# Attention: the order of the operations inside a step, on TensorE and on the engines that serve it

## What is computed

```python
qkv = x @ qkv_w.T + qkv_b
q = _apply_rope(q, cos, sin); k = _apply_rope(k, cos, sin)
logits = jnp.einsum('bqhmd,bkhd->bhmqk', q, k) * SM_SCALE        # 256 x 256 per head, masked to the window
w = e / (jnp.sum(e, axis=-1, keepdims=True) + exp_sink)          # e = exp(logits - max)
out = jnp.einsum('bhmqk,bkhd->bqhmd', w, v).reshape(Bv, Tv, N_HEADS * HEAD_DIM)
return out @ out_w.T + out_b
```

## Time and profile before

| | us |
|---|---|
| median of three runs | 1990.8 |
| the profiled execution | 1991.15 |
| its span in the profile | 1989.3 |
| a window of sweep 0 (305.40 to 352.10, unit of step 3 to unit of step 3) | 46.70 |
| a window of sweep 1 (905.36 to 951.85, the same L834 instruction) | 46.49 |
| TensorE busy over the span | 1945.1 (98%) |
| VectorE, ScalarE, GpSimd busy | 1549.4, 932.2, 826.0 |

### The profile page before, as it was taken

One profiled execution on the slowest core, in us unless ns is written; L12 is line 12 of the kernel. 1 busy time (PEld: TensorE's weight loads), 2 busy tenths in 40 slices (PEclk: granted clock), 3 DMA queues, 4 the chain that ended last, 5 costly groups with the idle time before them and its releaser, 6 DMA issues.

```text
span 1989.3 us, 44846 instructions
## 1 busy us (share of the span) xinstructions
PE 1945.1 (98%) x15500; PEld 1601.7 (81%) x15500; DVE 1549.4 (78%) x4948; ACT 932.2 (47%) x3481; POOL 826.0 (42%) x947
## 2 busy tenths in 40 slices
PE   6899999999999999999999999999999999999899
PEld 6688888888888888888888888888887777777687
DVE  5777777777777777777777777777777899999887
ACT  4554555555555555555555555555544222222333
POOL 3444434333333333333333333333332666666554
PEclk9999999999999999999999999999999999999999
DMA  6146211111112122121111111111104533333343
GB/s 213 46 118 142 72 54 55 65 54 55 55 54 75 44 97 76 55 89 62 54 55 54 54 54 55 54 65 54 54 33 167 183 103 93 93 93 93 106 142 121
DMA packets 71538, 162.20 MB, mean 82 GB/s; under 512 B 6656, under 2 KB 15232, under 8 KB 71184
## 3 DMA queue, kind: packets, MB, share of 16 engines
q1 hardware_dynamic: 62720, 142.48, 21.4%
q0 software_dynamic: 3840, 8.39, 2.3%
q10 hardware_dynamic: 4752, 8.46, 1.1%
HBM read 108.96 MB, written 50.41 MB: 80 GB/s over the span
## 4 chain that ended last, share of the span: by engine, by line
PE 91%; DVE 3%; issue 2%; ACT 2%; POOL 1%; DMA 0%; DVEq 0%; SPq 0%; ACTq 0%; POOLq 0%
PE banks L534 22%; PE banks L596 18%; PE banks L1180 16%; PE banks L573 9%; PE banks L549 9%; PE banks L559 6%; PE banks L1408 5%; PE banks L527 4%; ACT pr L673 1%; PE banks L484 1%; PE banks L1398 1%; PE banks L473 1%; PE banks L1392 1%; DVE pr L891 1%; DVE m L867 0%
## 5 line engine op out<-in xcount | busy, mean ns | idle before, releaser
L673 ACT ACTIVATE pr<-pr,mx 128x128 f32<-128x128 f32 x1024 | 399.0, 391 | 353.1 <-DVE mx L891 353.0
L752 POOL TENSOR_TENSOR m<-m,rope_sb 128x512 f32<-128x512 f32 x160 | 206.3, 1289 | 513.9 <-ACT m L660 513.9
L534 PE MATMUL banks<-xTh,wh 128*128 128x256 f32 x1280 | 376.4, 294 | 2.3 <-DVE xTl L851 1.4
L534 PE MATMUL banks<-xTl,wh 128*128 128x256 f32 x1280 | 363.0, 284 | 0.0
L534 PE MATMUL banks<-xTh,wl 128*128 128x256 f32 x1280 | 362.6, 283 | 0.0
L1180 PE MATMUL banks<-kv,tap 128*128 128x288 f32 x1280 | 318.4, 408 | 4.3 <-issue 1.5
L1180 PEld LDWEIGHTS banks<-kv,tap 128*128 128x128 f32 x1280 | 238.1, 190 | 83.9 <-issue 23.3
L534 PEld LDWEIGHTS banks<-xTh,wh 128*128 128x128 f32 x1280 | 246.2, 192 | 4.0 <-DVE xTl L851 1.8
L900 DVE TENSOR_TENSOR den<-ac,es 128x4 f32<-128x4 f32 x256 | 51.7, 202 | 253.9 <-ACT es L676 253.7
L534 PEld LDWEIGHTS banks<-xTl,wh 128*128 128x128 f32 x1280 | 246.5, 193 | 0.0
L534 PEld LDWEIGHTS banks<-xTh,wl 128*128 128x128 f32 x1280 | 246.1, 192 | 0.0
(11 more groups left out here) (110 smaller groups left out, 3825.6 us busy)
## 6 DMA issues: line engine op xcount, KB each, us to landing
tap<-padded_taps SPq DMA_DIRECT2D x64, 256.0 KB, 3.3
kk<-in_ctxt SPq DMA_DIRECT2D x64, 192.0 KB, 3.4
x_in<-in_x SPq DMA_DIRECT2D x16, 512.0 KB, 3.8
xt_split<-xTh SPq DMA_DIRECT2D x16, 512.0 KB, 2.6
xt_split<-xTl SPq DMA_DIRECT2D x16, 512.0 KB, 3.6
xb<-in_x SPq DMA_DIRECT2D x16, 512.0 KB, 4.6
factors<-in_factors POOLq DMA_DIRECT2D x8, 1024.0 KB, 8.6
x_part_rows<-x SPq DMA_DIRECT2D x16, 512.0 KB, 3.0
```

The costliest lines, as they stand in the source:

```text
L534: last = pe.matmul(bank[:, h * T:(h + 1) * T], w[:, n, c, h * P:(h + 1) * P], a[:, s, c, :], start=(c == 0 and i == 0), stop=(c == KD - 1 ...
L673: act.activation(pr[:, s, a, cols], pr[:, s, a, cols], ACT.Exp, bias=mx[:, s, i:i + 1], scale=-1.0, accum_out=ac[:, s, i:i + 1])
L752: pool.tensor_tensor(m2[:, s], m2[:, s], rope_sb[:, 1 if i == 0 else 0, 1:3], ALU.mult).then_inc(sin_ready, 1)
```

## The change

```diff
--- before.py
+++ after.py
@@ -279,6 +279,10 @@
 
     def unit_of(p, j):
         return UNIT_AT.get(2 * (p % 4) + j)
+
+    def begun(y, p):
+
+        return not (y.first and p < 4)
 
     def unit_bank(y, p, n):
 
@@ -605,21 +609,25 @@
         def body(y):
             for p in range(8):
                 for j in range(2):
+                    n = unit_of(p, j)
                     if y.here(p, 3):
                         p_transposes(y, p, j)
-                    n = unit_of(p, j)
-                    if n is not None and not y.drain:
+                    if n is not None and not begun(y, p):
                         unit(y, p, n)
-                    if x_next(y, p, j):
+                    if x_next(y, p, j) and not begun(y, p):
                         x_transposes(y.window(p) + 1, p % 4 - 1)
                     if j == 0 and y.here(p, 2):
                         scores(y, p)
                     u, jj = (p - 4, 1) if j == 0 else (p - 3, 0)
                     if y.here(u, 0):
                         pv(y, u, jj)
+                    if x_next(y, p, j) and begun(y, p):
+                        x_transposes(y.window(p) + 1, p % 4 - 1)
                     if x1_here(y, p, j) is not None:
                         x1_transposes(y.window(p) - 3, x1_here(y, p, j),
                                       (QM + 1) * 2 * B if y.drain else (QM + 1) * y.window(p) + 1 + p % 4)
+                    if n is not None and begun(y, p) and not y.drain:
+                        unit(y, p, n)
                     if y.drain and p == 3 and j == 1:
                         conv.first_products(pe)
                     for s in parts_of(y, p, j):
@@ -707,23 +715,25 @@
                     if y.here(p, 3):
                         p_evac(y, p, j)
                     n = unit_of(p, j)
-                    if n is not None and n != V_UNIT and not y.drain:
+                    if n is not None and n != V_UNIT and not begun(y, p):
                         bent(y, p, rope_index(n), unit_bank(y, p, n))
-                    if x_next(y, p, j):
+                    if x_next(y, p, j) and not begun(y, p):
                         x_high(y.window(p) + 1, (p // 4 + 1) % 2, p % 4 - 1, y.m + p // 4)
                     u, jj = (p - 4, 1) if j == 0 else (p - 3, 0)
-                    if y.here(u, 0):
+                    if y.here(u, 0) and (j == 0 or not begun(y, p)):
                         o_high(y, u, jj)
+                    if y.here(p, 2):
+                        exps(y, p, j)
+                    if y.here(u, 0) and j == 1 and begun(y, p):
+                        o_high(y, u, jj)
+                    if x_next(y, p, j) and begun(y, p):
+                        x_high(y.window(p) + 1, (p // 4 + 1) % 2, p % 4 - 1, y.m + p // 4)
                     if x1_here(y, p, j) is not None:
                         x1_evac(y.window(p) - 3, x1_here(y, p, j))
-                    if not y.first:
-                        for i, n in split_now(y, p, j):
-                            split_high(i, n)
-                    if y.here(p, 2):
-                        exps(y, p, j)
-                    if y.first:
-                        for i, n in split_now(y, p, j):
-                            split_high(i, n)
+                    if n is not None and n != V_UNIT and begun(y, p) and not y.drain:
+                        bent(y, p, rope_index(n), unit_bank(y, p, n))
+                    for i, n in split_now(y, p, j):
+                        split_high(i, n)
                 if y.drain and p in (4, 6):
                     conv.first_queries(act, p // 2 - 2)
                 if y.drain and p == 4:
@@ -781,18 +791,20 @@
             for p in range(8):
                 for j in range(2):
                     n = unit_of(p, j)
-                    if n is not None and n != V_UNIT and not y.drain:
+                    if n is not None and n != V_UNIT and not begun(y, p):
                         rotate(y, p, rope_index(n))
+                    if y.here(p, 2):
+                        if y.first and p == 2 and j == 0:
+                            pool.wait_ge(c_in, 16 * NCONST)
+                        sinks_shifted(y, p, j)
                     if p % 4 == 1 and j == 0 and not y.first and not late(y, 2, p):
 
                         pool.wait_ge(xb_landed, 16 * (y.window(p) - 1))
                         for t in range(NT):
                             last = pool.tensor_tensor(xb[:, t, :], xb[:, t, :], bo_sb[:], ALU.add)
                         last.then_inc(xb_ready, 1)
-                    if y.here(p, 2):
-                        if y.first and p == 2 and j == 0:
-                            pool.wait_ge(c_in, 16 * NCONST)
-                        sinks_shifted(y, p, j)
+                    if n is not None and n != V_UNIT and begun(y, p) and not y.drain:
+                        rotate(y, p, rope_index(n))
                     for i, n in split_now(y, p, j):
                         if y.first and n >= NU:
                             split_low(i, n)
@@ -965,15 +977,19 @@
                         conv.first_sums(dve)
                     if residual_tile(y, p, j) is not None:
                         residual(y, p, residual_tile(y, p, j))
+                    if j == 1 and begun(y, p) and y.here(p, 2):
+                        mask_min(y, p, j)
                     u, jj = (p - 3, 1) if j == 0 else (p - 2, 0)
                     if y.here(u, 0):
                         divide(y, u, jj)
                     if y.here(p, 3):
                         mask_transposed(y, p, j)
+                    if j == 0 and begun(y, p) and y.here(p, 2):
+                        mask_min(y, p, j)
+                    u, jj = (p - 4, 1) if j == 0 else (p - 3, 0)
+                    if y.here(u, 0) and begun(y, p):
+                        o_low(y, u, jj)
                     n = unit_of(p, j)
-                    early = 2 * (p % 4) + j in (1, 3) and not fresh(y, p) and not y.drain
-                    if early:
-                        mask_min(y, p, j)
                     if n is not None and not y.drain:
                         if y.first and n == V_UNIT and p < 4:
                             dve.wait_ge(c_in, 16 * NCONST)
@@ -983,10 +999,9 @@
                             turned(y, p, rope_index(n), unit_bank(y, p, n))
                     if x_next(y, p, j):
                         x_low(y.window(p) + 1, (p // 4 + 1) % 2, p % 4 - 1)
-                    if y.here(p, 2) and not early:
+                    if y.here(p, 2) and not begun(y, p):
                         mask_min(y, p, j)
-                    u, jj = (p - 4, 1) if j == 0 else (p - 3, 0)
-                    if y.here(u, 0):
+                    if y.here(u, 0) and not begun(y, p):
                         o_low(y, u, jj)
                     sl = 2 * (p % 4) + j
                     if sl in (4, 6) and x_after(y, p):
```

## The result

The changed kernel takes 2120.97 us in the median (2120.13 to 2122.66) against 1990.32: 1.0659 times the time before, 95% interval 1.0645 to 1.0672. The profiled execution is at 2120.13, 129.0 over the profiled one of before; the sum had said 117.

The account below looks back on a forecast made before the run. TensorE, busy 98% of the span, was taken as the bound. The sum 14 × 5.1 − 2 + 4 × 1.3 + 5 + 13 × 2.9 = 117 over 1991.15 gave 2108 us, range 2040 to 2140.

Parts of the forecast that it names:

- The short way from the key unit to the next: Shared bank, steps 0 to 1: next unit due after 4.29, bank read takes 5.10, so 0.81 wait a window.
- The hold of `rotate` on `divide`: VectorE beside GpSimd: `divide` is held until `rotate` ends, the next start at `bent` + 4.04, not + 2.82.
- The first rival: `rotate` doesn't hold `divide` on VectorE: 29 us of loss, 2020 us; chance 14%.
- The replay of a window: Steady sweep 0 window: units of steps 1, 3, 5 wait 2.77, 1.66, 1.02; window 51.79, 5.1 more than before.
- In step 7 the values' `v_evac` ... fits in 4.29: Step 7, bank of the values unit: `v_evac` needs 0.68 only and fits in the 4.29 to the next unit.
- Sweep 1: Windows of the second sweep: waits of 1.46 in step 1 and 1.6 in step 3; 49.40, 2.9 more each.
- The seams: TensorE, where one kind of matmul follows another: 8 us to gain over 32 windows, with PV 0.45 behind transposes.
- Window 1 has waits of its own that hide some: 2 off: Window 1: waits already there hide some of the new loss, so 2 us are taken off the sum.
- `split_high` behind `bent` ...; I take 5: Ten steps: `split_low`, first on VectorE in the next step, comes later; nothing or 1.2 each, taken as 5 us.
- The second rival: VectorE's chain also delays step 0's transposes and `o_low` before PV: about 1 per window in 27 windows, 2135 us; 11%.

Follow-up runs that it names:

- e4: The changed kernel with VectorE's `mask_min` ahead of `divide` in even steps too; 2041.41 us, 1.0257 times before.
- e1: The changed kernel with `rotate`'s two GpSimd instructions cut from 512 to 4 columns a partition after the first body; 2045.62 us, 1.0278 times before.
- e9: e4, but PV of step 7 takes the values of the window before and waits for those alone; 2026.13 us, 1.0178 times before.
- e11: e4 with e7's two edits, output projection parts moved from step 7 to the next step 0 and from step 5 to step 6; 2001.09 us.
- e7: The changed kernel with window 1 in the old order and `split_high` ahead of `exps`; 2108.91 us, 1.0592 times before.
- e8: The kernel before, sweep 0's x transposes moved behind PV, `x_high` behind `o_high`, `x_low` behind `o_low`, from window 2 on; 2010.22 us, ratio 1.0098.
- e6: e4 with the old order in step 6 alone, on all engines; 2063.82 us, 1.0365 times before.
- e5: e4 with the old order in steps 0 and 6, on all engines; 2084.42 us, 1.0467 times before.
- e10: e4 with e7's two edits, output projection parts moved from step 1 to step 0 and from step 5 to step 6; 2026.96 us, 1.0181 times before.

## Why the prediction was right

The time lies in the range and 13 us above the value, 130.7 of loss where 117 was forecast. By its own steps:

- **The short way from the key unit to the next** (0.81): right. It is 0.81 in e4 and 0.83 in e1, where everything else is out of its way.
- **The hold of `rotate` on `divide`** (`bent` + 4.04): right, 4.00 in the trace. e1 takes it away and 75 us with it; e4 takes it away together with 1.6 of VectorE's queue, and 80 us. It is three products of eight that are held, not four: in step 2 it is `den`. The Trainium skill (GPSIMD Engine Reference, Key points) names contention between GpSimd and instructions of VectorE with two SBUF inputs, without a price; the trace of after agrees, with 1.63 for an instruction that takes 0.69 alone. The first rival falls.
- **The replay of a window:** waits of 2.77, 1.66 and 1.02 forecast, 1.98, 1.28 and 0.76 measured, and one of 0.46 that the replay didn't have. "In step 7 the values' `v_evac` ... fits in 4.29" looked at the unit of step 7 alone; PV of step 7 multiplies with this window's values and comes before that unit. e9 prices it at 15 us. `bent` of step 7 starts 0.31 before step 0 (309.08 against 309.39), not 0.38 after it, and these 0.69 make up most of the 0.79 by which the wait in step 1 is smaller. That the helpers catch up while TensorE stands at PV fits this, but was not tried. In sum 4.35 a window where I had 5.1.
- **Sweep 1:** waits of 1.46 and 1.6 forecast, 1.13 and 1.11 measured, and three that the replay didn't have: 0.46 at PV of step 7, 0.33 at PV of step 3, 0.2 at the transposes of step 2. In sum 3.36 a window where I had 2.9: the two named waits were too high, and what was left out made up for it.
- **The seams** ("8 us to gain"): mis-sized. Transposes to PV are 0.53, the upper bound, not 0.45; a unit behind PV is 2.97 and a part behind it 1.39, near enough. Taking the four waits from the window of sweep 0 leaves 46.58, and e11 says 46.67 in sweep 1 and 46.66 in sweep 0: no gain, where 8 us were in the sum.
- **"Window 1 has waits of its own that hide some: 2 off":** wrong in sign. Windows 0 and 1 lose 9.3, not 3.1. e7 returns it there, 4.2 of it not for good. The sum has no term for the granted clock, and up to 6 of the 9.3 can be that.
- **"`split_high` behind `bent` ...; I take 5":** too low. Windows 15 to 18 lose 20.7, against 10.2 with this term in it. The step that failed is that it was priced as `split_low`'s length in ten slack steps. In windows 16 and 18 the split stands in front of `divide` in step 0, at the head of the chain that reaches the unit of step 1, which starts 8.1 and 8.0 after the key unit. Then the clock falls, which adds 3.8. e7 returns 6 of the 20.7; how the rest divides between `split_low` and the clock was not tried.

The last two and windows 19 to 31 are low by about 23 in all, with 2 at the end, windows 2 to 14 high by about 13. The loss was right to 12% partly by luck: errors of both signs met.

The second rival (transposes of step 0 and `o_low` late as well) did not come as it was put: the transposes of step 0 don't wait in steady windows, and `mask_transposed` waits are 14.5 in the whole kernel, 11.9 before. A half of it is there in sweep 1, though, with PV of step 3 waiting for `o_low` and the transposes of step 2 late, 0.5 a window. Not tried: a second bank for the units, since the kernel uses all eight of its banks.

## What to carry to other kernels

In a pipeline written out by hand, measure for every shared bank the time from its last write to its next, and compare it with the whole path that frees it, the queue ahead of each instruction on that path included; an order that saves a seam of 0.1 us can shorten that time by 1.5. Then look at what each pair of VectorE and GpSimd instructions will newly run beside: here a product of two SBUF operands on VectorE that landed beside a GpSimd sum of 1.27 us ended 0.55 after it and took 1.63 instead of 0.69, and moving one independent piece between them (e4), which also shortens the path, gave back 80 us. And a small piece of work between two others may be the cover of a wait (e8): before it is moved, ask what the instruction behind it would have waited for. And when waits are added, read the granted clock of the stretch before its whole loss is put down to waits.

## What the runs showed that I had not expected

- Orders that match are worth far more than their difference. Each side of the change alone costs 346 to 400 us, a part of it at the lower clock, both together 131: with one set of score banks and one bank for PV, TensorE's order and VectorE's must agree on whether `mask_min` and `o_low` or the unit come first.
- Steps are not independent either. Putting one step of eight back (e6) cost 22 us, two (e5) 43.
- Cover of 1.4 us in the right place does more than most of the reordering: moving two parts of the output projection takes e4's window in sweep 1 from 48.14 to 46.67 (e11), but taking one of the two from step 1 instead of step 7 leaves 47.71 (e10).
